# Two cross attentions on one core: a unit's four heads are transposed together behind the fourth keys product, in the logits' PSUM banks

## What is computed

```
kh = concatenate([kv_in @ wk + bk, bias_k])            # 376 keys per batch and head
vh = concatenate([kv_in @ wv + bv, bias_v])
logits = einsum('bqhk,bthk->bhqt', qh, kh) / sqrt(128)
weights = softmax(logits, axis=-1)
ctx = einsum('bhqt,bthk->bqhk', weights, vh)
return ctx @ wo + bo
```

## Time and profile before

| | us |
|---|---|
| median of 3 runs | 3082.3 |
| the profiled execution, whole | 3077.73 |
| its span in the trace | 3076.4 |
| PE busy | 2936.4 (95%) |
| PE weight loads busy | 2473.7 (80%) |
| DVE busy | 1296.4 (42%) |
| ACT busy | 1137.2 (37%) |
| POOL busy | 1031.3 (34%) |

### The profile page before, as it was taken

The page is one execution under the profiler, slowest core; times in us unless marked ns, Lnnn a source line. Parts: engine busy times, 40 slices in busy tenths (PEclk is TensorE's granted clock), DMA queues, the critical chain, the costliest instruction groups (busy, mean ns, idle before and its releaser), DMA issues.

```text
span 3076.4 us, 43508 instructions
## 1 busy us (share of the span) xinstructions
PE 2936.4 (95%) x16396; PEld 2473.7 (80%) x16396; DVE 1296.4 (42%) x3064; ACT 1137.2 (37%) x2639; POOL 1031.3 (34%) x988
## 2 busy tenths in 40 slices
PE   6999998799999999999999999999999999988999
PEld 3564566788989898888989999989888877777887
DVE  5775776443333333333333333333421156563134
ACT  2343344443442233333222232233343355564332
POOL 4665574222231122222121131121245333346420
PEclk8898999999999999999999999999999999999999
DMA  6765661433332122222221222221111111111132
GB/s 218 211 216 175 197 197 62 153 124 139 130 135 86 56 94 75 74 75 78 75 76 73 74 95 74 74 89 61 55 42 69 67 46 46 44 32 67 55 117 96
DMA packets 120829, 301.56 MB, mean 98 GB/s; under 512 B 17040, under 2 KB 71824, under 8 KB 111792
## 3 DMA queue, kind: packets, MB, share of 16 engines
q1 hardware_dynamic: 120144, 298.09, 28.5%
q10 hardware_dynamic: 480, 0.69, 0.1%
HBM read 268.60 MB, written 30.15 MB: 97 GB/s over the span
## 4 chain that ended last, share of the span: by engine, by line
PE 82%; DVE 6%; ACT 5%; issue 3%; POOL 3%; DMA 0%; PEld 0%; PEldq 0%; SPq 0%; POOLq 0%; ACTq 0%; DVEq 0%
PE bank L192 23%; PE bank L194 22%; PE bank L193 22%; PE bank L1918 6%; PE bank L1903 2%; PE bank L682 2%; POOL W_lo L232 1%; PE bank L2588 1%; DVE max L2135 1%; DVE prob L2802 1%; ACT prob L2009 1%; PE bank L621 1%; ACT prob L2706 1%; ACT W_hi L223 1%; PE bank L2602 1%
## 5 line engine op out<-in xcount | busy, mean ns | idle before, releaser
L2219 POOL TENSOR_SCALAR prob<-prob,inverse 112x376 f32<-112x376 f32 x256 | 143.6, 580 | 1228.8 <-DVE inverse L2141 1228.8
L192 PE MATMUL bank<-ctx_hi,W_hi 128*128 128x376 f32 x1024 | 355.5, 347 | 22.2 <-issue 12.0
L232 POOL TENSOR_TENSOR W_lo<-W_raw,W_hi 128x1024 fp32r<-128x1024 f32 x138 | 328.7, 2404 | 108.3 <-ACT W_hi L223 104.8
L274 DVE SCALAR_TENSOR_TENSOR K_lo<-bank,vectors,K_hi 128x375 fp32r<-128x375 f32 (+1 forms) x288 | 173.0, 606 | 408.8 <-ACT K_hi L265 408.8
L193 PE MATMUL bank<-ctx_lo,W_hi 128*128 128x376 f32 x1024 | 344.8, 337 | 0.0
L194 PE MATMUL bank<-ctx_hi,W_lo 128*128 128x376 f32 x1024 | 344.4, 336 | 0.0
L192 PE MATMUL bank<-act_hi,W_hi 128*128 128x448 f32 x784 | 296.4, 378 | 2.5 <-issue 1.0
L2009 ACT ACTIVATE prob<-bank,minus 112x376 f32<-112x376 f32 x256 | 143.4, 573 | 402.9 <-DVE minus L2138 402.9
L193 PE MATMUL bank<-act_lo,W_hi 128*128 128x448 f32 x784 | 290.1, 370 | 0.0
L194 PE MATMUL bank<-act_hi,W_lo 128*128 128x448 f32 x784 | 289.9, 370 | 0.0
L265 ACT ACTIVATE K_hi<-bank,vectors 128x375 fp32r<-128x375 f32 (+1 forms) x288 | 163.0, 577 | 254.5 <-PE bank L194 254.4
(11 more groups left out here) (282 smaller groups left out, 6060.8 us busy)
## 6 DMA issues: line engine op xcount, KB each, us to landing
W_raw<-in_weights SPq DMA_DIRECT2D x69, 1024.0 KB, 4.9
ctx_hi<-ctx_split SPq DMA_DIRECT2D x64, 752.0 KB, 4.3
ctx_lo<-ctx_split SPq DMA_DIRECT2D x64, 752.0 KB, 5.9
v_spread<-v_rows SPq DMA_DIRECT2D x88, 224.0 KB
values<-value_rows SPq DMA_DIRECT2D x32, 256.0 KB
V<-values SPq DMA_DIRECT2D x16, 512.0 KB, 4.0
att<-in_ctxT SPq DMA_DIRECT2D x16, 376.0 KB, 5.7
ctx_split<-W_hi SPq DMA_DIRECT2D x16, 376.0 KB, 3.8
```

The source lines that it names most:

```text
L192: nc.tensor.matmul(dst, left[0], right[0], start=first, stop=False)
L232: pool.tensor_tensor(k.Wl[:, slot, cs, :], k.Wraw[:, cs, :], k.Wh[:, slot, cs, :].bitcast(F32), ALU.subtract).then_inc(*k.w_low.now((n, i)))
L274: dve.scalar_tensor_tensor(out=low, in0=src, scalar=bias, in1=high.bitcast(F32), op0=ALU.add, op1=ALU.subtract).then_inc(*k.banks.draining ...
L2219: pool.tensor_scalar(k.Pm[:, h, :], k.Pm[:, h, :], k.rsum[:, h:h + 1], 1.0, ALU.mult, ALU.mult).then_inc(*k.prob_done.now((n, h)))
```

## The change

The four turns of a unit stand together behind K3, in both kinds of units. They no longer take banks 0 to 3 but banks 4 to 7: t(n, h) goes into the bank of L(n, h), whose exponential has drained it. The copies out of them move on ACT and DVE behind their last K_hi and K_lo. The number of instructions on each engine stays as it was.

```
@@ unit_steps
     for h in range(1, HK):
-        steps += [("K", n, h)] + ([("t", n - 1, h - 1)] if n else [])
-    steps += [("t", n - 1, HK - 1)] if n else []
+        steps += [("K", n, h)]
+    steps += [("t", n - 1, h) for h in range(HK)] if n else []
     steps += [("turn", *turns_of(n))] if turns_of(n) else []
@@ plan_xattn
-    keys = [s for n in range(len(UNITS)) for s in unit_steps(n) if s[0] != "L"]
+    keys = [s for n in range(len(UNITS)) for s in unit_steps(n) if s[0] not in ("L", "t")]
     n = len(UNITS)
-    keys += [("t", n - 1, h) for h in range(HK)] + [("turn", 2, NR - 2), ("pv", n - 1), ("xo", n - 1), ("turn", 2, NR - 1)]
+    keys += [("turn", 2, NR - 2), ("pv", n - 1), ("xo", n - 1), ("turn", 2, NR - 1)]
     u.rotate(keys, [0, 1, 2, 3], two=("K", "pv", "turn"))
     for n in range(len(UNITS)):
         for h in range(HK):
             u.use(("L", n, h), 4 + h)
+            u.use(("t", n, h), 4 + h)
@@ act_xattn
             act_high(k, key, k.Kh[:, h, 0:S], k.banks.tile(key)[:, 0:S], V(k, f"bk{gg // G + 1}", gg % G * HK + h))
-            if n and h == 2:
-                act_prob_turned(k, n - 1, 1)
         if n:
+            act_prob_turned(k, n - 1, 1)
             act_prob_turned(k, n - 1, 3)
@@ dve_xattn
-            if n and h == 1:
-                dve_prob_turned(k, n - 1, 0)
             if turn and h == 2:
                 dve_norm_out(k, *turn)
         if n:
+            dve_prob_turned(k, n - 1, 0)
             dve_prob_turned(k, n - 1, 2)
```

## The result

The changed kernel took 3059.6 us, the median of 4 runs (3059.03 to 3060.42), beside 3081.9 us for the kernel before on the same chip (3081.41 to 3083.11). The ratio is 0.9928, with a 95% interval of 0.9916 to 0.994: 22.3 us faster, where 20.1 were forecast. The time lies in the range (3054 to 3075), 2.6 us under the forecast of 3062.2.

The account below looks back on a forecast made before the run. PE was taken to bound the kernel (82% of the chain). Terms -0.9, -7.1, -5.4, 0, +3.1 and -11.3 gave -21.6 us, -20.1 after the clock correction: 3082.3 to 3062.2 us, range 3054 to 3075.

Parts of the forecast that it names:

- step 2: 13 units behind a weight split: t1's wait for K0's bank goes; -0.55 us each, -7.1 us.
- step 3: 8 units with a turn: V0's wait for K3's bank behind the turn goes; -5.4 us.
- step 6: Made units 5, 7, 13, 15 and 6, 10, 14: K2's long waits for K0's bank shrink; -11.3 us.
- Step 1: All 63 units: three groups of transposes become one block of twelve, linear at 1.09 us; -0.04 us each, -0.9 in 23 plain units.
- Step 4: 4 units with split and turn: the turn still waits for the normalised tile, so nothing gained; 0 us.
- Step 5: Made units 1 to 4, 8, 9, 11, 12: L0 newly waits for DVE's copy of t0; +3.1 us.
- The correction for the clock: Units with split and turn: longer stretch without ordinary matmuls, one clock fall charged among four; +1.5 us, -21.6 becoming -20.1.
- A: Rival: as forecast, with none to two falls of the clock; 3058 to 3066 us; chance 0.66.
- B: Rival: clock falls in all four split-and-turn units and about a third of the made ones; 3074 us; chance 0.17.
- C: Rival: block of twelve at pv's pace or below, clock falling at each made unit; 3112 us; chance 0.03.
- D: Rival: gains handed on as waits for POOL, ACT or the context; about 3084 us; chance 0.06.
- E: Rival: block runs at the pace of its first three transposes, no clock falls; 3048 us; chance 0.08.

Follow-up runs that it names:

- Experiment 1: Changed kernel with the turns still grouped behind K3 but back in banks 0 to 3 of the rotation; 3104.9 us.
- experiment 2: Changed kernel with turns and their copies back between the keys, in the old order, but in banks 4 to 7; 3053.5 us.
- experiment 6: Kernel of experiment 3 with POOL's root ahead of its split of the queries in the 12 units with a turn; 3045.2 us.
- experiment 7: Kernel of experiment 6 with POOL also waiting for the normalised tile before splitting the queries, in the 12 units with a turn; 3042.3 us.
- Experiment 3: Changed kernel with DVE copying t0 ahead of the last K_lo instead of behind it; 3047.7 us.
- experiment 4: The kernel before, unchanged, profiled a second time; one run, 3084.5 us.
- Experiment 5: Changed kernel with each turn's transposes issued four times over in the 48 units with V, 48 in a row instead of 12; 3218.9 us, one run.

## Why the prediction was right, step by step

**The four corners.** Order and banks can be set apart:

| us | turns in banks 0 to 3 | turns in banks 4 to 7 |
|---|---|---|
| turns between the keys | 3082.3 (before) | 3053.5 |
| turns behind K3 | 3104.9 | 3059.6 (after) |

There is no gain without the new banks, and the grouping costs time in either column: 22.6 us in the old banks, 4.0 (by the stage) to 6.1 (by the medians, of two chips) in the new ones. The prediction priced the two together and did not part them.

Unit by unit it is less simple. The waits that steps 2, 3 and 6 name come from the rotation of banks 0 to 3, as they say, and they go when no t takes its place in it between the keys, whichever of the two edits sees to that. Experiment 1 loses them as well: units 5, 7, 13 and 15 gain there what they gain in after, t1 waits no more, and V0 stands 0.38 us behind the turn's start. What the old banks cost in the grouped order is one other wait, t3's for the bank of K3, in all 63 units (41.8 us), and that is what the new banks save there.

**Step 1, twelve transposes in a block.** Linear as taken: 1.08 or 1.09 us up to V0, and 1.15 where a turn's transposes stand behind. The bounds of 0.88 and 1.45 us were both wide of it. From K0 to V0 a plain unit takes 9.35 us (9.39 before; forecast 9.35). The 0.07 us gained per unit, against 0.04, includes 0.02 us in V0 and as much in V1, for which I have no cause.

**Steps 2 and 3, the waits behind a split and behind a turn.** -0.53 and -0.68 against -0.55 and -0.68. The cause was the place of t in the rotation: experiments 1 and 2 both lose the two waits, but with the turns in banks 0 to 3 another comes, at t3. Two readings of the prediction were loose without harm: V0 comes 2.6 us and not 4 us behind the old t1, and the 0.35 for a turn's four transposes is not 4/3 of 0.29, which is 0.39; 0.36 was measured.

**Step 4, split and turn together.** The mechanism held: the wait for the normalised tile went from 1.16 to 1.69 us in unit 29. The 2.3 forecast for it was a slip: PE is done with the keys 0.62 + 0.51 = 1.13 us earlier, but the block behind them is 0.58 us longer than the six were, and 1.16 + 1.13 - 0.58 = 1.7. The turn stands where it stood, 11.26 us behind the unit's start (11.27 before). That the unit gained 0.2 all the same was missed: it came behind the turn, where V0 starts 0.41 us later instead of 0.61. Before, V0 took K3's bank here too, and DVE was only just done with it in unit 29:

```profile
1285.58 0.60 DVE L274 SCALAR_TENSOR_TENSOR K_lo<-bank,vectors,K_hi 128x375 fp32r<-128x375 f32 x1
```

This K_lo ends 0.14 us ahead of V0's start (1286.32 in the earlier trace rows). It is step 3's wait over again, short enough to bear no mark of its own. Experiments 6 and 7 confirm that the wait for the normalised tile hung on POOL's order.

**Step 5, the new wait in made units.** The wait came where it was said, with L0 at E + 2.15 instead of E + 2.21, and pv at E + 3.23 (forecast 3.24). The regular units lost 0.29 to 0.35 us instead of 0.40, for a reason that was not in the sum: pv, which now waits for nothing, takes 2.60 instead of 2.67 us. Experiment 3 removed the wait and got 0.71 to 0.83 back per unit, so it was this wait and no other.

**Step 6, the long waits.** -11.3 us as forecast; that it fits to a tenth is partly luck, for units 7 and 15 gave 0.1 more than said and units 6, 10 and 14 0.2 less in sum. In unit 13 the clock no longer fell, and K3 waited 0.58 us for its bank (forecast 0.7). Some 4.4 us of the sum are the three falls of the clock in the profile of before. Against the execution of experiment 4, which has a fourth, unit 5 gains 2.99 us and not 1.42.

**The correction for the clock.** This is the term that missed. I charged one fall of the clock in the four units with both, +1.5 us; none came in the profiled execution. The step was wrong in kind: it set the whole stretch without ordinary matmuls (3.6 us forecast, 3.4 measured) against unit 13's 2.8 us of waiting, as if a transpose were a wait. Experiment 5 shows that PE kept 1.00 through 4.96 us of transposes, and experiment 1 that 2.55 us of waiting inside the stretch lost it. Without the term the forecast would have been 3060.7.

**The rivals.** It came out as A, with no fall in the stage. B and C fell with the result and with experiment 5. D, gains handed on, occurred only where step 4 had it, in the four units with both; all others kept what they had gained. E needed a block quicker than linear, and there was none.

## What to carry to other kernels

When an edit both reorders steps and moves their buffers, run the two apart and compare stretch by stretch: here one was worth 28.8 us and the other cost between 4 and 23, though either alone removed the longest waits. A short step that takes a buffer in a rotation waits for what stood there a full turn earlier; put it into buffers that are idle just then, and see which row must empty them before their next user. And a wait that stays can be one row's place on a helper's queue: moving one row of DVE gave back 0.7 to 0.8 us in each of 14 units, and moving one of POOL and holding back another 1.1 us in each of four.

## What the runs showed of the hardware

- Transposes of 112 columns (fp32, against an identity) follow each other at 0.096 us in a row of 48, and TensorE's granted clock stays at 1.00 (2.4 GHz) throughout; of twelve waits of 2.32 to 2.56 us (four each in the profiles of before, experiment 1 and experiment 4) eleven came with a fall to 0.50 (1.2 GHz) and one did not; of the sixteen waits of 1.32 to 1.70 us in the stage of after and of experiments 2, 3 and 6 none did.
- A tensor_scalar of 128x512 on DVE took 1.27 us when it began 0.15 us behind a tensor_tensor of 128x448 on POOL, 1.06 us when it began 0.38 us behind it, and 0.55 us when it began ahead of it; in the first two cases it ended 0.28 us behind POOL's end.
- Twenty-four matmuls of pv take 2.60 us when PE arrives at them without a wait and 2.67 behind one.
